# The middle blocks of a language-model tower: lags, who adds, and how expert weights are mixed

## The reference, cut to what matters

```python
# feed-forward: fake quantization to integers, scale from the largest absolute value
xq = _act_fake_quant(x, clip_x[0])
gate = einsum('bsh,ih->bsi', xq, _weight_fake_quant(w_gate))
up = einsum('bsh,ih->bsi', xq, _weight_fake_quant(w_up))
h = _act_fake_quant(silu(gate) * up, clip_down[0])
out = einsum('bsi,hi->bsh', h, _weight_fake_quant(w_down))

# recurrence: eight experts' weights mixed per sequence
x = inputs * rsqrt(mean(inputs * inputs, -1) + EPS) * norm_weight
probs = softmax(mean(x, axis=1) @ router_w.T + router_b)
W_hg = einsum('be,ekd->bkd', probs, w_hg)
W_out = einsum('be,eod->bod', probs, w_out)
hidden, gate = split(einsum('bsd,bkd->bsk', x, W_hg))
h = exp(log of the scan h[t] = (1 - s(gate)) h[t-1] + s(gate) g(hidden))
out = einsum('bsk,bok->bso', h, W_out) + inputs

# h = h + layer(_layernorm(h)) around each of them
```

## Time and profile before

| | us |
|---|---|
| median of 3 runs | 4301.55 |
| the profiled execution itself | 4291.31 |
| its span | 4289.4 |
| busy in the span: PE, DVE, ACT, POOL | 4058.3, 3115.0, 2681.0, 1969.9 |
| `feed_forward` | 1076.9 to 1207.0 |
| `recurrence` | 1207.3 to 1288.4 |
| first DMA of the local layers' block | 1289.57 |

### The profile page before, as it was taken

One profiled execution on the slowest core, in us unless ns is written; L12 is line 12 of the kernel. 1 busy time (PEld: TensorE's weight loads), 2 busy tenths in 40 slices (PEclk: granted clock), 3 DMA queues, 4 the chain that ended last, 5 costly groups with the idle time before them and its releaser, 6 DMA issues. The chain is left out here.

```text
span 4289.4 us, 98138 instructions
## 1 busy us (share of the span) xinstructions
PE 4058.3 (95%) x33209; PEld 2830.0 (66%) x33212; DVE 3115.0 (73%) x5389; ACT 2681.0 (63%) x7061; POOL 1969.9 (46%) x1362
## 2 busy tenths in 40 slices
PE   6999979999567999999999999999999999999997
PEld 3666546665234777777777777777777777777776
DVE  4888548887686777777777777677777777777774
ACT  3677536776425666666666666666666666666664
POOL 1000000000235665666665656566656666566662
PEclk8999989999679999999999999999999999999999
DMA  6111142220102000210011101110011100111001
GB/s 156 38 43 44 24 120 65 55 54 15 59 20 92 21 20 19 61 39 21 19 52 41 31 16 24 47 52 18 21 35 44 43 19 21 48 47 25 21 20 49
DMA packets 103319, 177.61 MB, mean 41 GB/s; under 512 B 27317, under 2 KB 61905, under 8 KB 102737
## 3 DMA queue, kind: packets, MB, share of 16 engines
q1 hardware_dynamic: 102096, 169.70, 14.8%
q0 software_dynamic: 768, 2.10, 0.4%
HBM read 94.93 MB, written 23.07 MB: 28 GB/s over the span
## 5 line engine op out<-in xcount | busy, mean ns | idle before, releaser
L2160 POOL TENSOR_TENSOR swp<-raw,table 128x512 f32<-128x512 f32 x384 | 481.1, 1274 | 663.0 <-DVE ss L2571 662.8
L938 DVE TENSOR_REDUCE maxima<-PS 128x1 f32<-128x512 f32 x1024 | 632.4, 681 | 123.7 <-PE PS L772 123.3
L2243 PE MATMUL PS<-wqk,xT 128*128 128x512 f32 x1536 | 688.9, 601 | 5.7 <-DMA wqk<-in_L_ffn_Wqkv 4.4
L2190 POOL TENSOR_TENSOR probs<-probs,prob_recip 128x512 f32<-128x512 f32 x384 | 475.5, 1257 | 432.6 <-DVE prob_recip L2629 432.6
L902 ACT ACTIVATE probs<-PS 128x512 f32<-128x512 f32 x1024 | 520.2, 602 | 154.6 <-PE PS L786 153.9
L2500 ACT ACTIVATE probs<-probs,neg 128x128 f32<-128x128 f32 x1536 | 595.9, 389 | 27.1 <-DVE neg L2623 25.6
L2170 POOL TENSOR_TENSOR rinv<-ssm,power 128x32 f32<-128x32 f32 x96 | 525.8, 5477 | 0.0
L2243 PEld LDWEIGHTS PS<-wqk,xT 128*128 128x128 f32 x1536 | 283.8, 190 | 338.3 <-issue 254.6
L2346 PE MATMUL PS<-xnT,w 128*128 128x128 f32 x3840 | 479.9, 276 | 0.4 <-DVE hidden L2689 0.4
L772 PE MATMUL PS<-k_stack,q_stack 112*128 112x512 f32 (+1 forms) x1024 | 430.6, 442 | 35.4 <-PEq L640 19.9
L2346 PEld LDWEIGHTS PS<-xnT,w 128*128 128x128 f32 x3840 | 455.2, 193 | 1.4 <-issue 0.7
(11 more groups left out here) (275 smaller groups left out, 8210.9 us busy)
## 6 DMA issues: line engine op xcount, KB each, us to landing
V_window<-V SPq DMA_DIRECT2D x180, 256.0 KB, 2.8
wqk<-in_L_ffn_Wqkv SPq DMA_DIRECT2D x12, 1024.0 KB, 6.4
w<-in_L_ffn_W SPq DMA_DIRECT2D x18, 640.0 KB
q_stack<-spin_qk SPq DMA_DIRECT2D x128, 80.0 KB
k_stack<-spin_qk SPq DMA_DIRECT2D x128, 80.0 KB
q_stack<-tok_qk SPq DMA_DIRECT2D x128, 64.0 KB, 2.7
k_stack<-tok_qk SPq DMA_DIRECT2D x128, 64.0 KB, 2.8
spin_qk<-shared SPq DMA_DIRECT2D x32, 256.0 KB
```

Source lines behind the costliest of these rows:

```text
L938: dve.tensor_reduce(maxima[:, k // 2, k % 2:k % 2 + 1], SM(r, k), AX.X, ALU.max).then_inc(sm_maxed, 1)
L2160: pool.tensor_tensor(swp[:, w, :, a:a + LD // 2], raw[:, w, :, b:b + LD // 2], table[:, j % 2, 2 + w, a:a + LD // 2].rearrange("p (o d) -> ...
L2190: pool.tensor_tensor(view, view, psr[:, 4 * q:4 * q + 4].rearrange("p (h o) -> p h o", o=1) .to_broadcast([P, 4, P]), ALU.mult).then_inc(p ...
L2243: mm = pe.matmul(wide(kind, half, j), xT[:, k, at:at + P], rhs, start=(k == 0), stop=(k == DC - 1))
```

## The change

In `feed_forward`: DVE clips all four chunks of X in front. ACT and POOL start with other instructions (a Silu of one column; the two small memsets ahead of the large one). In the down loop DVE clips pair g+1 before it scales pair g, ACT rounds g+1 and converts g+2, PE turns pair g-3 instead of g-2, and DVE takes g-4 instead of g-3. DVE, not POOL, adds the scaled output into H, right behind the scaling, and counts in the same step. norm_weight is multiplied in when RT is written, by two instructions that replace the copy; `share_norm` is gone. Exponentials and shares of sequence 0 come at the end.

In `recurrence`: W_out of sequence 0 is mixed on PE, as matmuls with eight diagonals of the shares that DVE writes first, and copied by ACT; sequence 1 is mixed by ACT and POOL as before (seven sums). `mix` takes both row blocks in one instruction of 128x512. The final norm is on ACT with an offset from POOL.

```diff
         scaled_out = c.sb(ctx, "scaled_out", [P, 2, PAIR, D])
@@ -1332,18 +1332,13 @@
 
             @block.gpsimd
             def _(pool):
-                pool.memset(hT[64:P, IC - 1, :], 0.0).then_inc(cleared, 1)
-                pool.wait_ge(cleared, 1)
                 pool.memset(power[:, :], -0.5).then_inc(cleared, 1)
                 pool.memset(ones[:, :], 1.0).then_inc(cleared, 1)
+                pool.wait_ge(cleared, 2)
+                pool.memset(hT[64:P, IC - 1, :], 0.0).then_inc(cleared, 1)
...
-                def add_output(g):
-                    pool.wait_ge(out_scaled, g + 1)
-                    at = slice(PAIR * g, PAIR * g + PAIR)
-                    pool.tensor_tensor(c.H[:, at, :], c.H[:, at, :], scaled_out[:, g % 2, :, :], ALU.add).then_inc(ffn_added, 1)
...
                 for g in range(PAIRS + 1):
                     if g < PAIRS:
-                        add_output(g)
                         deviations(g)
                     if g:
                         join(g - 1)
...
-                for g in range(PAIRS + 2):
+                for g in range(PAIRS + 3):
                     if g < PAIRS:
                         down(g)
-                    if g >= 2:
-                        turn_normed(g - 2)
-                    if g == PAIRS // BATCH + 2:
+                    if g >= 3:
+                        turn_normed(g - 3)
+                    if g == PAIRS // BATCH + 3:
                         logits(0)
...
+                act.activation(table[:, :], c.ident[:, 0:1], ACT.Silu)
...
                 to_integers(0)
+                to_integers(1)
+                round_h(0)
                 for g in range(PAIRS + 2):
                     if g + 1 < PAIRS:
-                        to_integers(g + 1)
-                    if g < PAIRS:
-                        round_h(g)
+                        round_h(g + 1)
+                    if g + 2 < PAIRS:
+                        to_integers(g + 2)
                     if g >= 2:
                         norm_again(g - 2)
-                    if g == PAIRS // BATCH + 3:
-                        exponentials(0)
+                exponentials(0)
                 exponentials(1)
...
+                def add_output(g):
+                    at = slice(PAIR * g, PAIR * g + PAIR)
+                    dve.wait_ge(out_scaled, g + 1)
+                    dve.tensor_tensor(c.H[:, at, :], c.H[:, at, :], scaled_out[:, g % 2, :, :], ALU.add).then_inc(ffn_added, 1)
...
                 def take_normed(g):
                     dve.wait_ge(r_turned, g + 1)
-                    dve.tensor_copy(x.RT[:, :, PAIR * g * P:PAIR * (g + 1) * P], c.PS[:, 2 + g % 2, :].rearrange("p (k t) -> p k t", k=DC)).then_inc(r_taken, 1)
+                    for k in range(DC):
+                        ins_ = dve.tensor_scalar(x.RT[:, k, PAIR * g * P:PAIR * (g + 1) * P], c.PS[:, 2 + g % 2, PAIR * k * P:PAIR * (k + 1) * P],
+                                                 nw[:, k:k + 1], None, ALU.mult)
+                    ins_.then_inc(r_taken, 1)
...
-                clip_x(1)
+                for ch in range(1, CHUNKS):
+                    clip_x(ch)
...
                             largest(ch, 0)
-                        if j == 4 and ch + 2 < CHUNKS:
-                            clip_x(ch + 2)
                     largest(ch, 1)
...
-                for g in range(PAIRS + 3):
-                    if g < PAIRS:
-                        clip_h(g)
-                    if 1 <= g <= PAIRS:
-                        count(g - 1)
+                clip_h(0)
+                for g in range(PAIRS + 4):
+                    if g + 1 < PAIRS:
+                        clip_h(g + 1)
                     if g < PAIRS:
                         scale_output(g)
+                        add_output(g)
+                        count(g)
                     if 1 <= g <= PAIRS:
                         norm(g - 1)
-                    if g >= 3:
-                        take_normed(g - 3)
-                    if g == PAIRS // BATCH + 2:
+                    if g >= 4:
+                        take_normed(g - 4)
+                    if g == PAIRS // BATCH + 3:
                         mean_of(0)
-                    if g == PAIRS // BATCH + 3:
+                    if g == PAIRS // BATCH + 4:
                         logits(0)
-                    if g == PAIRS // BATCH + 4:
-                        shares(0)
                 mean_of(1)
                 logits(1)
+                shares(0)
                 shares(1)
...
                 pool.memset(power[:, :], -0.5).then_inc(power_set, 1)
-                for b in range(BATCH):
-                    for e in range(1, E):
-                        n = (E - 1) * b + e - 1
-                        pool.wait_ge(multiplied, E * b + e + 1)
-                        if n:
-                            pool.wait_ge(summed, n)
-                        pool.tensor_tensor(x.mixed_out[:, b, :, :], x.mixed_out[:, b, :, :], product[:, n % 2, :, :], ALU.add).then_inc(summed, 1)
+                for e in range(1, E):
+                    pool.wait_ge(multiplied, e + 1)
+                    wait(pool, summed, e - 1)
+                    pool.tensor_tensor(x.mixed_out[:, 1, :, :], x.mixed_out[:, 1, :, :], product[:, e % 2, :, :], ALU.add).then_inc(summed, 1)
...
+                    pool.wait_ge(shift_done, 4 * ch + 1)
+                    pool.tensor_tensor(rstd[:, at], shifted[:, at], power[:, at], ALU.pow).then_inc(shift_done, 1)
+                    pool.wait_ge(shift_done, 4 * ch + 2)
+                    pool.tensor_tensor(offset[:, 0, at], moments[:, at, 0], rstd[:, at], ALU.mult).then_inc(shift_done, 1)
+                    pool.wait_ge(shift_done, 4 * ch + 3)
+                    pool.tensor_scalar(offset[:, 1, at], offset[:, 0, at], -1.0, None, ALU.mult).then_inc(shift_done, 1)
...
+                def blend_output():
+
+                    pe.wait_ge(diag_ready, 1)
+                    for e in range(E):
+                        pe.wait_ge(x.out_loaded[e], 16)
+                    for k in range(DC):
+                        for e in range(E):
+                            mm = pe.matmul(c.PS[:, 4, k * D:(k + 1) * D], diag[:, e, :], x.wout[:, e, k, :], start=(e == 0), stop=(e == E - 1))
+                    mm.then_inc(blended, 1)
+
                 def hidden_gate(n):
                     b, o = units[n]
-                    pe.wait_ge(mixed_in, E * DC * (n + 1))
+                    pe.wait_ge(mixed_in, E * (n + 1))
                     wait(pe, hg_step, 2 * (n - 2) + 1)
+                    if n == 1:
+                        pe.wait_ge(blend_taken, 1)
...
+                blend_output()
...
+                        dst = product[:, e % 2, :, :]
+                    act.activation(dst, x.wout[:, e, :, :], ACT.Copy, scale=x.share[:, 1, e:e + 1]).then_inc(multiplied, 1)
+
+                def norm(ch):
+                    act.wait_ge(shift_done, 4 * ch + 4)
+                    for t in range(4 * ch, 4 * ch + 4):
+                        act.activation(c.X[:, t, :], c.H[:, t, :], ACT.Identity, bias=offset[:, 1, t:t + 1], scale=rstd[:, t:t + 1]).then_inc(normed, 1)
...
-                for e in range(E):
-                    weigh_output(0, e)
+                act.activation(table[:, :], c.ident[:, 0:1], ACT.Sigmoid)
+                for e in range(E // 2):
+                    weigh_output(e)
+                act.wait_ge(blended, 1)
+                act.activation(x.mixed_out[:, 0, :, :], c.PS[:, 4, :].rearrange("p (k d) -> p k d", k=DC), ACT.Copy).then_inc(blend_taken, 1)
                 sigmoids(0)
-                for e in range(E // 2):
-                    weigh_output(1, e)
-                sigmoids(1)
                 for e in range(E // 2, E):
-                    weigh_output(1, e)
-                sigmoids(2)
-                sigmoids(3)
+                    weigh_output(e)
+                for n in range(1, len(units)):
+                    sigmoids(n)
+                for ch in range(CHUNKS):
+                    norm(ch)
...
+                    dst = x.mixed[:, b, :, :].rearrange("p k (w i) -> p k w i", w=2)[:, :, :, o * P:(o + 1) * P]
                     for e in range(E):
                         if n == 0:
                             dve.wait_ge(x.hg_loaded[e], 16)
-                        for k in range(DC):
-                            at = E * DC * n + DC * e + k
-                            dst = x.mixed[:, b, k, :].rearrange("p (w i) -> p w i", w=2)[:, :, o * P:(o + 1) * P]
-                            src = x.whg[:, e, k, :].rearrange("p (w i) -> p w i", w=2)[:, :, o * P:(o + 1) * P]
-                            by = x.shareT[:, b, k, e:e + 1]
-                            if e == 0:
-                                dve.tensor_scalar(dst, src, by, None, ALU.mult).then_inc(mixed_in, 1)
-                            else:
-                                dve.wait_ge(mixed_in, at - DC + 1)
```

(39 more changed lines are left out.)

30 lines of the change are left out of this document (11 added, 19 removed).

## The result

| | us |
|---|---|
| after: median of 4 runs | 4238.80 (4237.10 to 4244.68) |
| before, run beside it: median of 4 runs | 4299.89 |
| ratio, 95% interval | 0.9861 [0.9844, 0.9878] |
| profiled execution after | 4244.68, span 4242.8 |

The change is 61 us faster by the medians and 46.6 by the two profiled executions.

The account below looks back on a forecast made before the run. Bounds: DVE in first part and recurrence, a chain across engines in the down loop. -4.2 - 18.9 - 6.8 = -29.9 us took 4291.3 to 4261.4; plus 10.2 to the median, 4271.6, range 4258 to 4285.

Parts of the forecast that it names:

- the rest shifts: Rival: the 3000 us behind the edited stretch depend on DMA starts and code position; +30 us would cancel the gain; chance 0.05.
- From profile to median: Whole kernel: 10.2 us added to 4261.4, because the median of runs, 4301.6, lay that far above the profiled execution.
- First part: Gate and up projections: two clips leaving the chunk loop give 2.9 us, the Silu table load 1.3; sum -4.2.
- memset 0 as taken: Front of feed_forward: POOL's moved memset might speed the first clip by 0 or about 1.6 us; 0 was taken.
- Down loop: Down projection: clipping a pair ahead breaks the chain; later steps 5.6 us, bound by low-clock PE; eighth scaling 21.7 us sooner.
- A PE busy all through the loop at 0.50: Down loop: listed among the signs that would show the forecast wrong, PE always busy at a clock of 0.50.
- hot PE: Rival: PE stays at the high clock through loop and tail; period 4.8, tail 15.6; about 4266 us; chance 0.12.
- blocking POOL: Rival: POOL blocks DVE wherever both work; down-loop period 8.3 us, second part gives 0.3; 4290.3 us; chance 0.09.
- Tail: Eighth scaling to block's end: grows from 14.5 us to 17.3, the middle taken of 19.6 (low clock) and 15.6 (high); +2.8.
- Recurrence: Recurrence: -6.1 us until the fourth unit's matmuls, mostly from seven fewer POOL adds, and -0.7 at the end; sum -6.8.
- The merging itself gives nothing: Recurrence: a mix unit merged into 128x512 instructions takes 6.0 us, against 6.06 before.
- The blend's own time: Recurrence: mixing W_out by matmuls on PE, 32 in the trace, takes 9.5 us; 14 if cold throughout.

Follow-up runs that it names:

- b_pad17: Kernel before plus 17 idle 1 x 1 matmuls (68 instructions) at the end of PE's list in the recurrence; 4277.8 us beside 4293.6 of before.
- a_undo: Changed kernel plus 187 idle PE instructions, putting the layer loop's jump 256 behind its place in the kernel before; 4257.2 us beside 4240.1 of the changed kernel.
- a_noclip: Changed kernel with clips, Silu table load and memset at the front of feed_forward as before; 4246.9 us beside 4240.0 of the changed kernel.
- b_loop: Kernel before with only the changed kernel's down loop; clips, tables, memset, copy of RT and recurrence as before; 4276.7 us beside 4293.6 of before.
- a_noblend: Changed kernel with both sequences' W_out mixed by ACT and POOL (14 additions), without diagonals and their PE matmuls; 4265.0 us.
- a_two: Changed kernel with sequence 1's W_out blended on PE too; 4237.7 us, and repeated on one chip 4234.4 beside 4240.1 of the changed kernel.
- b_rec: Kernel before with only the changed kernel's recurrence, and norm_weight multiplied in when RT is written; 4264.0 us beside 4295.6 of before.

## Why the prediction was wrong

**The step that failed** is the rival "the rest shifts". It named code position and then took it as a loss only, with 0.05, "nothing in the profile points there"; and the sum put all behind the stretch at nothing. Yet the waits of before showed 10.4 us of "issue" in four nearly equal pieces at the loop's jump, and a clock that fell to 0.50 to 0.60 behind each. That was a cost which any edit ahead of the loop could turn on or off. It is 18.6 us of local layers by the traces, 15.8 and 17.1 by the two direct runs (b_pad17, a_undo). With the stalls kept, the changed kernel took 4257.2 (a_undo), still 0.8 us below the range. So the position is the largest part of the miss, not all of it. Of the 31.2 us between the forecast gain (29.9) and the medians' (61.1), 18.6 are the jumps, 4.3 the edited stretch, and 8.3 are left, which lie in the base more than in the kernel ("From profile to median", below). The edited stretch's 34.2 us lie within the bounds of its three parts together (16.9 to 40.1).

**First part.** It gave 6.8 us, outside its bounds of 4.0 to 5.9. Clips and table gave 3.2 in the profile of a_noclip (4.2 forecast), memset 0 as taken. The rest, some 3.4 us, I put down to PE's clock, which differs there (PE busy, clock; before, then after):

```profile
1096.00:1104.00 8.00, 6.09 (x26) 0.79 0.24 74
1104.00:1112.00 8.00, 5.47 (x24) 0.81 0.00 0
```

```profile
1096.00:1104.00 8.00, 6.23 (x33) 1.00 0.84 268
1104.00:1112.00 8.00, 6.23 (x33) 1.00 0.00 0
```

a_noclip supports this: with the old front its clock stood at 1.00 from 1090 to 1120, and it needs 55.8 us there, where the seven other profiles with the old front need 57.6 to 59.7. In all seven the clock is at 0.79 between 19 and 27 us behind the first clip; in a_noclip and in all twelve with the new front it is at 1.00. So the steadier clock seems to come with the new front, most of the time; no run separates the two. b_loop, which doesn't touch this part, got 1.6 us there, with a clock that rose earlier (0.69 instead of 0.50 over 1084 to 1090), so as much can be chance. I had no term for the clock. Behind the new table load (1081.71, 1.28 us) the next activation starts at 1083.01; of the drain of about 1.38 us that the Trainium skill ("ScalarE: Activation LUTs", What ACT_TABLE_LOAD costs) adds, this trace again shows nothing.

**Down loop.** Right in mechanism and size: 22.6 for 21.7, late steps 5.46 for 5.6, PE the bound at the low level. (A PE busy all through the loop at 0.50 was named as a sign of being wrong; it came in the late steps and was what the sum itself had counted on.) Neither the hot PE nor the blocking POOL came; in 4 of the 14 profiles with this loop the clock was higher for a part of it, and the eighth scaling came 1.1 to 1.9 us sooner. The Trainium skill's rule that POOL shares its SBUF interfaces with DVE ("GPSIMD Engine Reference", Key points) holds for small operands too, by the trace, but from POOL's side: its product of 128x2 took 0.20 us (at 1161.89) or, beside DVE's clip, 1.06 (at 1160.75). On DVE the price never reached the period.

**Tail.** +3.6 for +2.8, between the two bounds, near the low clock as it ran at 0.59. The sum had a slip here: the middle of 15.6 and 19.6 is 17.6, not 17.3, so +3.1. That loop and tail together give exactly the forecast 18.9 is luck: two misses of 0.8 cancel.

**Recurrence.** -7.9 for -6.1, but its parts were wrong. "The merging itself gives nothing" fell: a_noblend, which has the merged mixes and all 14 additions, needs 41.7 us to the fourth unit where b_loop, with the old ones, needs 44.8. Alone a merged unit takes 5.9 us and two halves 6.1. So the price of POOL's additions differs: a_two, which has none, is at its fourth unit after 32.6 us, of which 1.2 are the diagonals and 1.1 a wait, so 30.3 without both; 14 additions cost a_noblend 11.4 us above that, 0.8 each, and b_loop 13.9 above 30.9 (with unmerged units), 1.0 each. So merging gave 3.1 us, and the blend 4.9 instead of 5.8. These are differences between profiles; no run has the merging alone, and the Sigmoid table's load differs too. The blend's own time was right: 9.38 for 9.5.

**From profile to median.** I added 10.2 us since the median lay that far above the profiled execution. This was the second term that failed. The base of 4301.6 came from 3 executions; before took 4291.8 to 4295.6 in the later runs (4303.4 once). And median and profiled execution don't move together: the profiled execution of after was its slowest, that of before (4291.3) lies below all its others. Part of this is the unedited front: the first clip comes between 1076.6 (a_noclip) and 1086.1 us (b_rec) in the 18 profiles taken here, with the same code ahead of it.

## What to carry to other kernels

Before predicting an edit ahead of a rolled loop, look in PE's waits for "issue" at the loop's jump: if it is there, any change in the number of instructions ahead of the loop may remove it (or bring it in, if it isn't), and here a row of idle matmuls removed it at no cost that the traces show. A comparison of two versions holds this part too, so compare the unedited stretches apart. Next, an addition of 128x512 on POOL cost a busy DVE 0.8 to 1.0 us here; a matmul with diagonals on an idle PE saved it.

## What was not expected of the hardware

A stall of 2.7 us at the jump, four times, costs 4.65 us each on average, since the granted clock then stays at the low level for some 3 us (0.58 over 3.4 us). It depends on the code's place, and the old place came back after 256 instructions: of the places tried, the old one and those 3, 11 and 35 below stall, and those 1, 4, 16, 68, 69 and 133 above don't. How far below the bad stretch reaches stays open. So does the same question for the other engines: DVE, ACT and POOL each wait on "issue" four times, 6.4 to 9.1 us in all, in every run, whether PE stalls or not.
